# Linear attention with routed experts: 1/std by logarithm and exponential, and the keys of four batches in the first stage

## What is computed

```python
def _layernorm(x, axis=-1, eps=1e-05):
    m = jnp.mean(x, axis=axis, keepdims=True)
    v = jnp.var(x, axis=axis, keepdims=True)
    return (x - m) / jnp.sqrt(v + eps)
...
        q = _feature_map((x @ Wq.T).reshape(b, n, H, HD))
        k = _feature_map((x @ Wk.T).reshape(b, n, H, HD))
        v = (x @ Wv.T).reshape(b, n, H, HD)
        kv = jnp.einsum('bnhd,bhdm->bhdm', k, v)
...
        assign = jnp.argmax(aff, axis=1)
```

## Time and profile before

| quantity | us |
|---|---|
| median of three runs | 171.39 |
| lowest and highest of them | 169.41, 172.38 |
| the profiled execution's own time | 170.78 |
| its span, first to last instruction | 169.1 |

### The profile page before, as it was taken

One profiled execution on the slowest core, in us unless ns is written; L12 is line 12 of the kernel. 1 busy time (PEld: TensorE's weight loads), 2 busy tenths in 40 slices (PEclk: granted clock), 3 DMA queues, 4 the chain that ended last, 5 costly groups with the idle time before them and its releaser, 6 DMA issues.

```text
span 169.1 us, 4618 instructions
## 1 busy us (share of the span) xinstructions
PE 139.1 (82%) x1106; PEld 128.8 (76%) x1106; DVE 113.6 (67%) x411; ACT 104.9 (62%) x332; POOL 101.0 (60%) x108
## 2 busy tenths in 40 slices
PE   0066698999976987888799798999999999999950
PEld 0055597899944865766799688999999999999940
DVE  3899776999964865869756565666676665555540
ACT  8487996999252763556365647666676765566520
POOL 7600000899675655466235461888788868777884
PEclk9999999999999999999999999999999999999998
DMA  4999100680038765153234784698888878844433
GB/s 136 322 301 386 43 0 0 216 297 4 4 94 254 223 193 144 40 136 65 82 96 150 200 252 154 158 176 171 180 167 161 168 166 183 150 70 40 44 33 31
DMA packets 19113, 24.05 MB, mean 142 GB/s; under 512 B 2576, under 2 KB 13328, under 8 KB 18960
## 3 DMA queue, kind: packets, MB, share of 16 engines
q1 hardware_dynamic: 13456, 19.50, 36.2%
q0 software_dynamic: 5632, 4.26, 19.9%
HBM read 17.40 MB, written 6.36 MB: 140 GB/s over the span
## 4 chain that ended last, share of the span: by engine, by line
PE 53%; DVE 19%; issue 7%; ACT 7%; POOL 6%; another core or an unknown queue 2%; DMA 2%; DVEq 1%; ACTq 0%
PE bank L623 18%; PE bank L611 18%; POOL out L354 6%; PE bank L579 5%; PE bank L569 2%; ACT xn L401 2%; PE bank L596 2%; PE bank L515 2%; DVE feat_q L886 2%; PE bank L506 2%; PE bank L587 2%; DVE lane_neg L810 2%; PE bank L603 2%; DMA x<-in_x 2%
## 5 line engine op out<-in xcount | busy, mean ns | idle before, releaser
L470 ACT ACTIVATE hT<-bank,b 128x128 f32<-128x128 f32 x156 | 44.5, 368 | 29.6 <-PE bank L611 25.7
L354 POOL DMA_INDIRECT out<-rows,token_at x32 | 50.0, 1563 | 15.1 <-DVE rows L925 9.0
L346 POOL DMA_INDIRECT rows<-z_rows,token_at x32 | 30.6, 958 | 25.0 <-PE bank L611 11.5
L623 PE MATMUL bank<-w,hT 128*128 x312 | 42.8, 280 | 3.2 <-ACT hT L470 1.8
L623 PEld LDWEIGHTS bank<-w,hT 128*128 128x128 f32 x312 | 37.8, 191 | 5.2 <-issue 4.9
L611 PE MATMUL bank<-zT,feat_k 128*128 128x128 f32 x312 | 41.2, 275 | 0.0
L611 PEld LDWEIGHTS bank<-zT,feat_k 128*128 128x128 f32 x312 | 37.9, 192 | 0.0
L362 POOL TENSOR_TENSOR feat_k<-feat_k,k_exp 128x256 f32<-128x256 f32 x16 | 14.4, 920 | 24.8 <-ACT k_exp L449 24.3
L912 DVE TENSOR_SCALAR zT<-xn,ln_g,ln_b 128x128 f32 x39 | 13.7, 352 | 8.7 <-issue 7.6
L925 DVE SCALAR_TENSOR_TENSOR rows<-y_own,weight,rows 128x128 f32 x39 | 13.7, 351 | 7.7 <-DVE y_own L919 4.4
L579 PE MATMUL bank<-kv_all,feat_q 128*128 128x144 f32 x64 | 11.4, 300 | 6.9 <-DVE feat_q L886 5.5
(11 more groups left out here) (111 smaller groups left out, 228.9 us busy)
## 6 DMA issues: line engine op xcount, KB each, us to landing
feat_k<-in_w1T SPq DMA_DIRECT2D x39, 256.0 KB
z_rows<-xn SPq DMA_DIRECT2D x4, 528.0 KB, 5.8
w<-in_w2T SPq DMA_DIRECT2D x1, 2048.0 KB, 10.9
out<-x SPq DMA_DIRECT2D x8, 256.0 KB
x<-in_x SPq DMA_DIRECT2D x2, 768.0 KB, 7.0
x<-in_x SPq DMA_DIRECT2D x2, 256.0 KB, 2.9
b<-in_b SPq DMA_DIRECT2D x1, 512.0 KB, 6.5
rows<-z_rows,token_at POOLq DMA_INDIRECT x32
```

The costliest lines, as they stand in the source:

```text
L346: g.indirect_dma_start(out=rows[:, t, :], out_offset=None, in_=z_dram, in_offset=bass.IndirectOffsetOnAxis(ap=token_at[:, t:t + 1], axis=0 ...
L354: g.indirect_dma_start(out=out_rows, out_offset=bass.IndirectOffsetOnAxis(ap=token_at[:, t:t + 1], axis=0), in_=rows[:, t, 0:D], in_offset ...
L470: last = a.activation(hT[:, par, c * P:(c + 1) * P], bank[hidden_bank(s)][:, c * P:(c + 1) * P], ACT.Relu, bias=b1[:, c, bass.ds(e, 1)])
L623: last = t_.matmul(bank[y_bank(s)][:, 0:D], hT[:, par, c * P:(c + 1) * P], w2[:, bass.ds(e * (FC * D) + c * D, D)], start=(c == 0), stop=( ...
```

## The change

- **1/std.** The two square roots of a chunk become Ln (with epsilon as a bias from a small tile) and Exp with scale -0.5 on ACT, for the first norm alone (`rough_rstd`). DVE makes one Newton step of three instructions. The `shift` tile goes away. The second norm's Ln and Exp are made once for all 32 tiles (`rough_rstd_2`), and `second_norm` follows `choose(0)` with its own Newton step.
- **Who normalises.** ACT normalises nothing. Of each group of four tiles DVE does three and POOL one.
- **Keys.** Values of batches 2 and 3 and the keys of batches 0 to 3 are issued on PE ahead of the third group's transposes; the four `exp_of_k` run on ACT in the first stage. Twelve remain in the middle stage. The PSUM banks of the first four keys and of the key-value products are chosen so that they don't collide.
- **ACT's order.** The second chunk's `rough_rstd` stands behind the copies of four batches of values. The warm-up at the top is an exponential, and the one at L432 is gone.

```diff
-            def sqrt_of(c):
+            def rough_rstd(c):
+
                 part = slice(CHUNK[c], CHUNK[c + 1])
                 act.wait_ge(var_ready, c + 1)
-                a.activation(std[:, :, part], var_e[:, :, part], ACT.Sqrt).then_inc(std_ready, 1)
+                a.activation(log_var[:, part], var[:, part], ACT.Ln, bias=eps_ln[:, 0:1]).then_inc(log_ready, 1)
+                act.wait_ge(log_ready, c + 1)
+                a.activation(rough[:, part], log_var[:, part], ACT.Exp, scale=-0.5).then_inc(rough_ready, 1)
+
+            def rough_rstd_2():
+
+                act.wait_ge(var_2_ready, 1)
+                a.activation(log_2[:, :], var_2[:, :], ACT.Ln).then_inc(log_2_ready, 1)
+                act.wait_ge(log_2_ready, 1)
+                a.activation(rough_2[:, :], log_2[:, :], ACT.Exp, scale=-0.5).then_inc(rough_2_ready, 1)
...
             act.wait_ge(rows_ready, 1)
-            a.activation(warm[:, :], lane_row[:, 0:1], ACT.Sqrt)
+            a.activation(warm[:, :], lane_row[:, 0:1], ACT.Exp)
             expand_lanes()
-            sqrt_of(0)
-            normalise(0)
-            normalise(1)
+            act.wait_ge(eps_ready, 1)
+            rough_rstd(0)
             copy_xnT(0)
             copy_xnT(1)
-            sqrt_of(1)
-            copy_v(0)
-            copy_v(1)
-            normalise(2)
-            normalise(3)
-            for gr in range(2, NG + LAG):
+            for b in range(K_FIRST):
+                copy_v(b)
+            rough_rstd(1)
+            exp_of_k(0)
+            exp_of_k(1)
+            copy_xnT(2)
+            exp_of_k(2)
+            for gr in range(3, NG + LAG):
                 if gr < NG:
                     copy_xnT(gr)
                 if gr == 3:
-                    sqrt_of(2)
-                    a.activation(warm[:, :], mean[:, 0:1], ACT.Exp, scale=0.0)
-                if gr + 2 < NG:
-                    normalise(gr + 2)
+                    rough_rstd(2)
                 for j in range(TG // TB):
                     copy_v((gr - LAG) * TG // TB + j)
+                if gr == 3:
+                    exp_of_k(3)
+                if gr == 6:
+                    rough_rstd_2()
```

On PE, and on DVE:

```diff
             for gr in range(NG):
+                if gr == K_FIRST * TB // TG:
+                    for b in range(K_FIRST - TG // TB, K_FIRST):
+                        values(b)
+                    for b in range(K_FIRST):
+                        project_k(b)
                 transpose_x(gr)
...
-                step(v_.reciprocal(rinv[:, :, 0:n], std[:, :, part]), filling)
-                step(v_.tensor_tensor(nw_a[:, :, 0:n], rinv[:, :, 0:n], rinv[:, :, 0:n], ALU.mult), filling)
-                step(v_.tensor_tensor(nw_b[:, :, 0:n], nw_a[:, :, 0:n], var_e[:, :, part], ALU.mult), filling)
-                step(v_.tensor_scalar(nw_a[:, :, 0:n], nw_b[:, :, 0:n], -0.5, 1.5, ALU.mult, ALU.add), filling)
-                step(v_.tensor_tensor(rstd[:, :, part], rinv[:, :, 0:n], nw_a[:, :, 0:n], ALU.mult), filling)
-                v_.scalar_tensor_tensor(shift[:, part], mean[:, part], -1.0, rstd[:, 0, part], ALU.mult, ALU.mult).then_inc(rstd_ready, 1)
+                v_.tensor_scalar(var_half[:, part], var[:, part], -0.5, -0.5 * EPS_LN, ALU.mult, ALU.add)
+                next(filling, None)
+                dve.wait_ge(rough_ready, c + 1)
+                step(v_.tensor_tensor(nw_a[:, 0:n], rough[:, part], rough[:, part], ALU.mult), filling)
+                step(v_.tensor_tensor(nw_b[:, 0:n], nw_a[:, 0:n], var_half[:, part], ALU.mult), filling)
+                v_.scalar_tensor_tensor(rstd[:, part], nw_b[:, 0:n], 1.5, rough[:, part], ALU.add, ALU.mult).then_inc(rstd_ready, 1)
```

More of the change, by code:

```diff
@@ L42, in linear_attention_and_routed_experts @@
     K_BANKS = 4
+    K_FIRST = 4
     TOKENS_AT = 10
@@ L108, in linear_attention_and_routed_experts @@
         stats = sb("stats", [P, NT, 6])
[L109 to L116, removed]
+        ms_a, ms_b = sb("ms_a", [P, 3, TC]), sb("ms_b", [P, TC])
+        mean, var, var_half = (sb(n, [P, NT]) for n in ("mean", "var", "var_half"))
+        log_var, rough = sb("log_var", [P, NT]), sb("rough", [P, NT])
+        nw_a, nw_b = sb("nw_a", [P, TC]), sb("nw_b", [P, TC])
+        rstd = sb("rstd", [P, NT])
+        var_2, var_2_half, log_2, rough_2, sq_2, nw_2, rstd_2 = (
+            sb(n, [P, NT]) for n in ("var_2", "var_2_half", "log_2", "rough_2", "sq_2", "nw_2", "rstd_2"))
         spread = sb("spread", [P, NT])
+        eps_ln = sb("eps_ln", [P, 1])
         warm = sb("warm", [P, 1])
@@ L341, in _, with normalise @@
             g.memset(xn[:, :, AT_ALPHA + 1:ZW], 0.0).then_inc(aug_ready, 1)
+            def normalise(gr):
+                pool.wait_ge(rstd_ready, chunk_of(gr * TG) + 1)
+                for t in range((gr + 1) * TG - XN_POOL, (gr + 1) * TG):
+                    last = g.tensor_scalar(xn[:, t, 0:D], x[:, t, :], mean[:, t:t + 1], rstd[:, t:t + 1], ALU.subtract, ALU.mult)
+                last.then_inc(xn_by_pool, 1)
+            for gr in range(NG):
+                normalise(gr)
             def gather(t):
@@ L395, in copy_xnT @@
                 a.activation(xnT[:, gr * TG * P:(gr + 1) * TG * P], bank[gr % 2][:, :], ACT.Copy).then_inc(xnT_ready, 1)
[L397 to L402, removed]
             def expand_lanes():
@@ L430, in _ @@
                 if gr == 3:
-                    sqrt_of(2)
-                    a.activation(warm[:, :], mean[:, 0:1], ACT.Exp, scale=0.0)
-                if gr + 2 < NG:
-                    normalise(gr + 2)
+                    rough_rstd(2)
                 for j in range(TG // TB):
                     copy_v((gr - LAG) * TG // TB + j)
+                if gr == 3:
+                    exp_of_k(3)
+                if gr == 6:
+                    rough_rstd_2()
             act.wait_ge(max_ready, len(CHOOSE) - 1)
             a.activation(alpha_e[:, :], aff_max[:, :], ACT.Exp, scale=-1.0).then_inc(sig_exp, 1)
[L441 to L451, removed]
+            for b in range(K_FIRST, NB):
                 exp_of_k(b)
@@ L545, in tokens @@
                 last.then_inc(tok_done, 1)
[L547 to L555, removed]
             def keys_values(b):
@@ L632, in _ @@
             for b in range(NB - 1):
-                if b + K_BANKS < NB:
+                if b >= K_FIRST and b + K_BANKS < NB:
                     project_k(b + K_BANKS)
@@ L697, in moments @@
                 v_.tensor_scalar(mean[:, part], ms_a[:, 0, 0:n], 0.5, None, ALU.mult)
[L698 to L702, removed]
+                step(v_.scalar_tensor_tensor(ms_b[:, 0:n], ms_a[:, 1, 0:n], 0.25, ms_a[:, 1, 0:n], ALU.mult, ALU.mult), filling)
+                v_.scalar_tensor_tensor(var[:, part], ms_a[:, 2, 0:n], 1.0 / D, ms_b[:, 0:n], ALU.mult, ALU.add).then_inc(var_ready, 1)
             def rsqrts(c, filling):
@@ L841, in owners @@
                 v_.tensor_tensor(own[:, :], row_ex[:, :], ex_f[:, :], ALU.is_equal).then_inc(own_ready, 1)
-            for c in range(len(CHOOSE) - 2):
+            choose(0)
+            second_norm()
+            for c in range(1, len(CHOOSE) - 2):
                 choose(c)
@@ L846, in _ @@
             v_.tensor_copy(token_half[:, :], token_no[:, :]).then_inc(starts_full, 1)
-            second_norm()
             choose(len(CHOOSE) - 2)
```

71 lines of the change are left out of this document (55 added, 16 removed).

## The result

| | us |
|---|---|
| kernel before, median of 4 runs | 170.7 |
| changed kernel, median of 4 runs (180.43 to 181.14) | 180.75 |
| ratio, changed to before | 1.058, 95% interval 1.053 to 1.063 |
| forecast | 181.0 (175.0 to 185.0) |

The kernel became 5.8% slower. The profiled execution has a span of 179.4 us, against 169.1.

The account below looks back on a forecast made before the run. The prediction took ACT, with its table loads, to pace the first stage and DVE's series the middle stage. From the profiled 170.78 us, plus 10.5, minus 0.5, it got 180.8 and forecast 181.0 us, range 175.0 to 185.0.

Parts of the forecast that it names:

- Nine loads: ACT, first stage: Ln and Exp each need their own table, seven loads more than before, 9.0 us of ACT time.
- Rival 1: ACT: one table serves Ln and Exp, no repeated loads; last copy of values at 28.9, total 171.4 us; chance 9%.
- No drain: ACT: a load costs only 0.02 us beside its length, not the skill page's drain of about 1.38 us per switch.
- First chunk: First stage: 1/std ready at 9.55, later by 1.05 us; first transposes start at 10.5, against 9.94.
- The load for Ln fits behind it, to 7.10: ACT, first chunk: Ln's table load runs right behind `expand_lanes`, which ends at 5.81, and is over at 7.10.
- POOL's tile: First chunk: POOL normalises its one tile of a group in 0.6 us, hidden beside DVE's three.
- Second chunk, and ACT as the pace: First stage: Ln and Exp behind four copies, ready at 19.95; then 18.3 us of ACT's list, last copy at 38.2.
- rival 4: Nine loads, and PE, idle up to 3 us twice, returns to long durations: 3 or 4 us more, 184.5; chance 6%.
- Rival 3: Nine loads, half of them hidden under waits for PE or DVE: 5.1 us less, 176; chance 14%.
- Last choice: End of DVE's choice of experts: about 10.5 us later, from 10.7 us less the shorter tail.
- Middle stage: From last choice to attention: DVE's series stays the bound and gains 0.5 us (0 to 1.2) from less company.
- POOL's additions now end some 4 us earlier relative to DVE: Middle stage: this frees two or three DVE instructions from POOL's company, 0.5 us.

Follow-up runs that it names:

- the two kernels with one load: Changed kernel with Exp in place of both Ln, ratio 1.010 to the kernel before; changed kernel with the table for Ln and Exp preloaded, 1.006.
- early Ln and Exp: Changed kernel, nine loads kept, second chunk's Ln and Exp moved ahead of the copies of the first four batches of values: ratio 1.058 to the kernel before.
- one table and early Ln and Exp: Changed kernel with the shared table preloaded and second chunk's Ln and Exp ahead of the four value copies: 0.994 (chip A), 0.990 (chip C) of the kernel before.

## Why the prediction was right

**Nine loads.** Right, at the four places, 1283 ns each. The upper bound of that term was the true one: the table fetched for Exp did not serve Ln, nor the one fetched for Ln the Exp behind it. The Trainium skill, "ScalarE: Activation LUTs", section "Table sets: the hidden batching unit", says that one set holds both exp and ln. The runs agree where that set is asked for by name ahead of the first activation (one load), and not where it isn't (nine). Rival 1 had its price right, though not its chance: it put the last copy without repeated loads at 28.9, and the two kernels with one load have it at 28.74 and 29.14.

**No drain.** Right: 0.01 to 0.03 us stand between a load and its neighbours wherever neither waits.

**First chunk.** 1/std at 10.07, forecast 9.55. The step that failed is "The load for Ln fits behind it, to 7.10". It started at 6.35, when DVE's variance came: in this place the load stood behind the wait. In the kernel before, the load at 0.81 stood ahead of its wait, and so did the one at 13.83 with early Ln and Exp. What decides it isn't shown.

**POOL's tile.** The term was mis-sized: 848 ns and not 600. It did not matter by itself, but DVE's first three tiles took 1.04 us beside it, where 0.9 was forecast, and the first transposes began at 11.23, not 10.5.

**Second chunk, and ACT as the pace.** The list of ACT's work was forecast to start at 19.95 and to take 18.3 us. It started at 20.64 on both chips and took 19.65 (to 40.29) on the first chip and 18.15 on the second. The difference went with TensorE's granted clock, 0.62 against 1.00 from 30 to 34.5 us. This is what rival 4 described, in a smaller size (1.5 us, not 3 to 4). Rival 3, half of the loads hidden, was wrong: in the changed kernel some 0.5 us of one load was, the third chunk's, which began at 25.14 while the variance came at 25.66.

**Last choice.** 41.92 and 40.23, forecast 40.2. The second value agrees by two errors that cancel: ACT's list began 0.7 us late, and the tail from the last copy to the last choice was 1.4 us (1.6 on the first chip) and not 2.0.

**Middle stage.** The size was right, the account of it only in part. Forecast: 0.5 us less than before, by less company on DVE. Measured: 18.2 against 18.6. From the last choice to the end of the last masking DVE was busy 16.20 of 17.45 us, against 17.17 of 17.84: 1.0 us less work, twice the forecast, of which 0.6 went into two waits. So "The key of batch 15 and its addition stand ahead of the last masking with room to spare" failed: the addition ended at 57.95, and DVE waited 0.34 and 0.24 us for PE's last products. So did "POOL's additions now end some 4 us earlier relative to DVE": the last one ended 16.0 us behind the last choice, against 16.4 before, since PE had waited 2.1 us for DVE's first masking. The stage is bound by DVE and PE together through that PSUM bank, and PE's share, 17.45 of 17.64 us busy, stood in the trace of before as plainly as DVE's.

**The end.** The attention stage began 11.9 us later, 1.9 more than the forecast had it; by that alone the profiled execution would have taken 170.78 + 11.9 = 182.7 us, not 181.14. The stages behind took 119.3 us and not 120.9. The two errors cancel, and the last 1.5 us of the agreement are luck. Why the later stages were shorter is not settled: on chip C four kernels that leave them alone show 119.6 to 120.8 us.

## What to carry to other kernels

A change of activation function in a loop is priced by the table: count the loads in the profile, and if two functions alternate, ask for the set that holds both before the first of them. A shorter part pays only where the stage waits for it; look for the wait (here a PSUM bank freed late by an instruction's place in another engine's order) before moving work. When the profile names one releaser of an instruction that waits for several, check that it had not been done long before.

## What was not expected of the hardware

- TensorE's granted clock fell to or near its 1.2 GHz level (0.50) in the first or the middle stage in several of these kernels, after pauses of 2.2 to 3.6 us, and not in others with a like pause. One and the same program did both: with one table and early Ln and Exp, after the same pause, the clock read 1.00 on chip A and 0.64 on chip C from 40 to 44 us. Which it is was worth 1.0 us there and up to 2.2 us between the traces of the middle stage. It makes a sum of a few tenths of a microsecond uncertain, however well its rows are read.
- The same program took 160.6 us on one chip and 170.6 on another (medians). Of the 11.1 us between their two traces, 9.2 lie behind the start of the attention stage.
- A `tensor_scalar` of 128x128 f32 with two scalar tiles took POOL 848 ns, nearly as long as its addition of 128x256 (905 ns).
